# Attention of a decoder layer: 24 instead of 22 head pairs' probabilities turned by DMA, and five steps moved around it

## The reference

```python
x = x + attn(layernorm(x))          # 16 heads of 128; RoPE, causal softmax over 128 keys
x = x + xattn(layernorm(x), k, fside, ctx)   # long convolution of v*ctx with k, skip term, times ctx
x = x + ffn(layernorm(x))           # top 4 of 16 experts (inter 176) and shared experts (704)

scores = einsum('bqnd,bknd->bnqk', Q, K) / sqrt(d_head);  scores = where(causal, scores, -inf)
z = einsum('bnqk,bknd->bqnd', softmax(scores), V);  out = einsum('bqnd,ndm->bqm', z, W_O) + b_O

kv = v[:, :, :, None] * ctx[:, :, None]       # 8 x 8 per group of 8 channels
y = causal_conv(kv, k) + kv * skip
out = einsum('bhijl,bhil->bhjl', y, ctx)
```

## Time and profile before

| | us |
|---|---|
| median of 3 runs (951.35 to 953.11) | 951.75 |
| the profiled execution, its own time | 951.14 |
| its span | 949.3 |
| PE busy / weight load / DVE / ACT / POOL | 896.7 / 797.7 / 789.2 / 454.7 / 502.1 |

### The profile page before, as it was taken

One profiled execution on the slowest core, in us unless ns is written; L12 is line 12 of the kernel. 1 busy time (PEld: TensorE's weight loads), 2 busy tenths in 40 slices (PEclk: granted clock), 3 DMA queues, 4 the chain that ended last, 5 costly groups with the idle time before them and its releaser, 6 DMA issues.

```text
span 949.3 us, 19283 instructions
## 1 busy us (share of the span) xinstructions
PE 896.7 (94%) x6129; PEld 797.7 (84%) x6129; DVE 789.2 (83%) x1706; ACT 454.7 (48%) x1227; POOL 502.1 (53%) x380
## 2 busy tenths in 40 slices
PE   6899999899999989999999999989998799999996
PEld 6798888788889878898887888877887699999985
DVE  6988877878888999788898977876779688888857
ACT  3656645545436564444565333462166244544430
POOL 1443424455554436777363677525718277777760
PEclk9999999999999999999999999999999899999999
DMA  7796371676546754765899575425255277787769
GB/s 271 258 356 232 130 284 72 186 203 144 157 134 189 206 162 133 180 173 179 263 297 290 158 206 133 139 79 221 69 201 161 76 128 131 129 131 132 127 117 310
DMA packets 137345, 169.59 MB, mean 179 GB/s; under 512 B 54944, under 2 KB 112160, under 8 KB 135968
## 3 DMA queue, kind: packets, MB, share of 16 engines
q1 hardware_dynamic: 122800, 149.31, 51.2%
q0 software_dynamic: 14448, 19.05, 12.1%
HBM read 100.52 MB, written 58.44 MB: 167 GB/s over the span
## 4 chain that ended last, share of the span: by engine, by line
PE 64%; DVE 15%; DMA 6%; issue 6%; POOL 4%; ACT 3%; SPq 1%; another core or an unknown queue 0%; DVEq 0%; POOLq 0%; ACTq 0%
PE bank L596 9%; PE bank L598 9%; PE bank L597 8%; PE bank L684 4%; PE bank L913 4%; PE bank L1023 4%; PE bank L710 3%; DVE turn L1612 3%; PE bank L712 3%; PE bank L711 3%; POOL xs L1446 2%; DMA prob_dram<-planes 2%; DVE rot L1633 2%; PE bank L886 2%; PE bank L888 2%
## 5 line engine op out<-in xcount | busy, mean ns | idle before, releaser
L1398 POOL TENSOR_TENSOR z_lo<-prob_t,z_hi 128x512 fp32r<-128x512 f32 x64 | 86.2, 1348 | 218.3 <-ACT z_hi L1257 194.0
L1612 DVE SCALAR_TENSOR_TENSOR turn<-bank,bqk,trig 128x1024 f32<-128x1024 f32 x128 | 161.1, 1276 | 35.5 <-PE bank L598 34.0
L1217 ACT ACTIVATE prob<-prob,negmax 128x128 f32<-128x128 f32 x256 | 99.4, 390 | 123.2 <-DVE negmax L1597 108.0
L1499 POOL DMA_INDIRECT sums<-ysb,token_at x79 | 123.3, 1561 | 57.3 <-DMA sums<-ysb,token_at 29.1
L1439 POOL TENSOR_TENSOR rot<-turn 128x512 f32<-128x512 f32 x64 | 95.2, 1488 | 44.4 <-DVE turn L1612 32.3
L596 PE MATMUL bank<-xt_hi,w_hi 128*128 128x512 f32 x256 | 109.3, 427 | 2.4 <-DVE xt_lo L1574 1.7
L598 PE MATMUL bank<-xt_hi,w_lo 128*128 128x512 f32 x256 | 100.8, 394 | 0.0
L597 PE MATMUL bank<-xt_lo,w_hi 128*128 128x512 f32 x256 | 100.5, 393 | 0.0
L1446 POOL DMA_INDIRECT xs<-xh,dest x64 | 73.7, 1151 | 41.2 <-DVE dest L1780 23.4
L1633 DVE TENSOR_TENSOR rot<-turn 128x512 f32<-128x512 f32 x64 | 92.2, 1480 | 0.0
L1468 POOL TENSOR_TENSOR kv<-c_t,v_t 128x512 f32<-128x512 f32 x60 | 70.5, 1202 | 20.2 <-ACT v_t L1179 11.5
(11 more groups left out here) (200 smaller groups left out, 2537.6 us busy)
## 6 DMA issues: line engine op xcount, KB each, us to landing
w_hi<-w_dram SPq DMA_DIRECT2D x24, 768.0 KB, 5.2
w_lo<-w_dram SPq DMA_DIRECT2D x24, 768.0 KB, 6.6
prob_dram<-planes SPq DMA_DIRECT2D x44, 256.0 KB
xe_all<-xs SPq DMA_DIRECT2D x79, 132.5 KB
wo_hi<-wo_dram SPq DMA_DIRECT2D x26, 256.0 KB, 5.3
wo_lo<-wo_dram SPq DMA_DIRECT2D x26, 256.0 KB, 6.3
sums<-zeros SPq DMA_DIRECT2D x3, 2176.0 KB, 9.6
raw<-in_wqkv SPq DMA_DIRECT2D x16, 384.0 KB, 4.2
```

The source lines that it names most:

```text
L1217: last = nc.scalar.activation(prob[h][:, b, :], prob[h][:, b, :], ACT.Exp, bias=negmax[:, h, b:b + 1], accum_out=total[:, h, b:b + 1])
L1499: nc.gpsimd.indirect_dma_start(sums_dram[s % SUMS], bass.IndirectOffsetOnAxis(ap=token_at[:, s:s + 1], axis=0), ysb[s % YBUFS][:], None, c ...
L1612: last = nc.vector.scalar_tensor_tensor(turn_all[m][:, 2 * i:2 * i + 2, :], qk_bank[2 * m + i][:].unsqueeze(1).to_broadcast([128, 2, GT]), ...
```

## The change

It has these parts:

1. **Two more pairs by DMA**, t = 7 (weighed in step 9) and t = 30 (weighed in step 32, the first of the drain).
2. **Loads behind the turns.** SP issues store, turn, store, turn, then the loads of w and wo.
3. **Skip sums.** The second goes into bank 1, after the projection of QE, instead of bank 5, and the first weighing at p = 3 follows it instead of the projection of QO. QO (bank 1) then waits until DVE has taken it. The wait of the weighing for the skip sums is gone.
4. **Second weighing.** In the steps p = 4 to 7 it comes after QE instead of after KE. In the steps p = 0 to 3 it stays behind KE.
5. **Low parts on POOL.** In steps by DMA head 1's low part comes before both rotations instead of between them.
6. **No wait for the scatters** on POOL (DVE's and SP's own waits for them stay).
7. **The drain step 32.** With pair 30 by DMA, ACT's exponentials of a head come before its weighed values, then a part of the shared experts' weights (`gus_high`); before, they came last. The turn back of the convolution's output (`cross_back`) is made before the scores on PE and added by DVE before the scores' maxima; DVE's low parts of the shared weights come later; SP loads the raw weights after the stores and turns of pair 30.

```diff
 def by_dma(t):
-    return PAIRS <= t < PAIRS * GROUPS - 2
+    return PAIRS - 1 <= t < PAIRS * GROUPS - 1
...
                     if by_dma(t):
-                        prob_store(t, 0)
+                        for h in range(2):
+                            prob_store(t, h)
+                            prob_turn(t, h)
                     if 0 < p < PAIRS - 1:
                         load_w(g, p + 1)
-                    if by_dma(t):
-                        prob_turn(t, 0)
-                        prob_store(t, 1)
-                    if 0 < p < PAIRS - 1:
                         load_o(g, p + 1)
-                    if by_dma(t):
-                        prob_turn(t, 1)
...
+            for h in range(2):
+                prob_store(PAIRS * GROUPS - 2, h)
+                prob_turn(PAIRS * GROUPS - 2, h)
             sp.wait_ge(wo_done, PAIRS * (GROUPS - 1) + W_BEFORE[0] - 1)
             load_wo(0)
             sp.wait_ge(v_ready, 2 * PAIRS * GROUPS)
...
                     pe.wait_ge(prob_landed[h], 16 * (dma_before(t) + 1))
                     if h == 0:
                         pe.wait_ge(v_taken, s * 2 - 2)
-                    if h == 0 and p == 3:
-                        pe.wait_ge(skip_taken, 2 * (s // PAIRS))
...
                 if p == 3:
-                    pe.wait_ge(zt_taken, s * 2 - 4)
                     cross_skip(h, 0, pt_bank)
-                    cross_skip(h, 1, zt_bank)
...
                 if h >= 0 and p == 3:
-                    if i < 2:
-                        pe.wait_ge(vt_taken, 2 * h + i + 1)
-                    elif i == 2:
-                        pe.wait_ge(skip_taken, 2 * h + 1)
+                    if i == 0:
+                        pe.wait_ge(vt_taken, 2 * h + 1)
+                    elif i < 3:
+                        pe.wait_ge(skip_taken, 2 * h + 3 - i)
...
-                    if live(2) and not by_pe and i == int(p == 3) and p < 4:
+                    if by_dma(s - 2) and p == 3 and i == 0:
+                        pe.wait_ge(vt_taken, 2 * g)
+                        cross_skip(g - 1, 1, banks[1])
+                    if by_dma(s - 2) and p < 4 and i == 0:
                         weigh_values(s, p, 0, first)
-                    if live(2) and not by_pe and i == 2:
+                    if by_dma(s - 2) and i == (2 if p < 4 else 0):
                         weigh_values(s, p, 1, first)
...
                         exps(h)
                         take_weighed(h)
                         weighed_high(h)
+                        if g == GROUPS:
+                            gus_high(h)
...
                 if late:
                     first_probs(s)
+                    z_low(s, 1)
                 for m in range(2):
-                    if late and m:
-                        z_low(s, 1)
...
                     ).then_inc(scattered[g], 16)
-                pool.wait_ge(scattered[g], 16 * hi)
...
                 if g == GROUPS and p == 0:
                     tokens_again(0)
-                    gus_low(0)
+                    cross_add(h - 1)
...
                 if p == 0 and g == GROUPS:
-                    cross_add(h - 1)
                     dve.wait_ge(back_added, 2 * (GROUPS - 1))
                     token_moments(2 * GB, 3 * GB)
+                    gus_low(0)
                     gus_low(1)
```

More of the change, by code:

```diff
@@ L73, in by_dma @@
 def by_dma(t):
-    return PAIRS <= t < PAIRS * GROUPS - 2
+    return PAIRS - 1 <= t < PAIRS * GROUPS - 1
 def dma_before(t):
-    return min(max(t - PAIRS, 0), PAIRS * (GROUPS - 1) - 2)
+    return min(max(t - PAIRS + 1, 0), PAIRS * (GROUPS - 1))
 def pe_before(t):
@@ L746, in between_weighings @@
                 s, h = g * PAIRS + p, g - 1
-                if p == 0 and g == GROUPS:
-                    two_banks_free(g, p, live)
-                    pe.wait_ge(v_taken, s * 2 - 1)
-                    cross_back(h - 1)
                 if g == 0 or not live(0):
@@ L892, in step @@
                     last.then_inc(wo_done, 1)
-                if p == 0 and 1 < g < GROUPS:
+                if p == 0 and g > 1:
                     two_banks_free(g, p, live)
                     pe.wait_ge(v_taken, s * 2 - 1)
-                    cross_back(h - 1)
+                    cross_back(g - 2)
                 beside_first(g, p, live)
@@ L1268, in step @@
                         h = i % 2
-                        if i == 1 and g == GROUPS and p < 2:
-                            if p == 1:
-                                root((g - 2) * GB, (g - 1) * GB)
-                            gus_high(2 * p)
-                            if p == 0:
-                                gus_high(1)
+                        if i == 1 and g == GROUPS:
+                            root((g - 2) * GB, (g - 1) * GB)
+                            gus_high(2)
                         if i == 3 and g == GROUPS and p == 1:
@@ L1921, in beside_scored @@
                     cross_skip(h, 0, pt_bank)
-                    cross_skip(h, 1, zt_bank)
+                    cross_skip(h, 1, banks[1])
                 if p >= 4:
```

## The result

The changed kernel takes 962.88 us (median of 8 runs, 959.58 to 967.62) against 953.82 for the kernel before (950.32 to 958.16), a ratio of 1.010 (95% interval 1.008 to 1.012): 1% slower, where 12 us less were forecast (range 935 to 948 us). Its profiled execution took 962.59 us, span 960.8; that of before is 11.5 us shorter. Single executions of one kernel lie several us apart, so times are compared by ratios and causes by the traces' own steps.

What follows compares the result with a forecast made beforehand. The prediction took PE as the bound, with DVE close behind. Its terms, -11.5 - 2.5 + 1.0 - 1.0 + 0.5 + 1.5 = -12.0 us, gave 939.1 us profiled, 939.7 median, range 935 to 948.

Steps and rivals of the forecast that it cites:

- What bounds the kernel: Groups 1 and 2: PE sets the pace, busy 157.1 of 162 and 154.8 of 160 us, DVE close behind.
- Loads behind the turns, no scatter wait, low part first, -11.5: Steps by DMA: PE's turn and output-sum stalls, 13.8 us, vanish; 11.5 us gained, bounds 5 to 13.8.
- The rule of the Trainium skill: DMA turns: 1309 ns per block against 390 on TensorE, 10.5 us a turn; the prediction trusted the trace's 3.23 us.
- Second weighing, -2.5 and +1.0: Steps p = 4 to 7: PE's wait before QO filled, 2.5 us gained; ACT slipping in some steps, 1.0 lost.
- Pair 7, -1.0: Pair 7 turned by DMA: two PE transpositions removed, 1.0 us gained, bounds 0 and 2.
- Skip sums, +0.5: At p = 3: QO waits for DVE's skip product instead of the weighing; 0.5 us lost, between 0 and 1.5.
- The drain, +1.5, at worst +5: Step 32 to the next output sum: 1.5 us lost, between a gain of 1 and a loss of 5.
- Rival C: Rotations: POOL and DVE hold each other up, 1.9 us a step, kernel 6 us slower, 958 us; chance 0.08.
- Rival A: DVE takes over: PE's gain mostly becomes waits for DVE; -7 us, 944.8 us; chance 0.22.
- B: Turns land no earlier: 8.5 us of stalls stay, about 7 of the 11.5 lost; 946.7 us; chance 0.05.

Runs made afterwards that it cites:

- b_mix2: Kernel before without POOL's scatter wait, the three zero fills moved ahead of group 1's steps, weight loads behind both turns; 941.50 us, ratio 0.988.
- a_drain: Changed kernel with its drain as before (pair 30 turned by TensorE, step 32 in its old order); 953.93 us, ratio to before 0.999.
- m_drain: b_mix2 with the changed kernel's drain (pair 30 by DMA, raw shared weights behind its turns); 953.65 us, ratio to before 1.002.
- b_mix: Kernel before without POOL's scatter wait and with the three zero fills moved ahead of group 1's steps; 947.09 us, ratio 0.992.
- m_low: b_mix2 with POOL's second low part ahead of both rotations; 951.60 us, ratio to before 0.999.
- a_fill: Changed kernel with the three zero fills issued in group 2 instead of group 3; 964.51 us, ratio to before 1.011.

## Why the prediction was wrong

- *What bounds the kernel.* Right that TensorE has the pace and DVE is close. Missed: POOL, busy for half of the time, has no room either from its division to its first kv. Its share of busy time hid that.
- *Loads behind the turns, no scatter wait, low part first, -11.5.* This step failed. It summed stalls that vanish, each from its own row, and took the covers as free. Measured one by one on before: loads +0.7%, no scatter wait -0.6%, low part +0.8%. The sentence "the rotations end at most as much later as the weighed values of head 1 come after the first rotation" had the delay right; it then looked only at the scores, and not at kv and the convolution behind the rotations. The sentence "the loads go out some 5 us later, for the next step" named no queue behind them: the next pair's store, the scattered rows, and the fills of group 3, which the prediction never named. Two of the three edits are a gain of 1.2% if the fills are moved as well and the low part stays. That these 12 us equal the forecast's sum is chance: they hold the fills, which it never named, and 2 us of the drain.
- *The rule of the Trainium skill* ("VectorE: DVE Perf Modes", The three transpose paths). The measured turns bear the row out, not the page's figure: in b_mix2 no turn of 22 pairs was waited for. What made a turn late was what lay in front of its store.
- *Second weighing, -2.5 and +1.0.* Failed: ACT did not slip, and zc's 3.0 us did go, but the steps p = 5 and 6 got 0.26 longer, since QO, now behind the weighing, brought DVE's reciprocals and with them POOL's division a quarter of a microsecond later. Alone it is worth nothing (1.001), on b_mix2 it costs 4 us.
- *Pair 7, -1.0.* No gain shows: steps p = 0 to 2 of group 1 took 50.17 us with it and without it.
- *Skip sums, +0.5.* Right in kind: QO waits for the same product. The size hangs on the clock: on b_mix2, where it fell behind the wait, step 32 began 1.7 us later; at a clock of 1.00 the p = 3 step of group 2 got 0.6 us shorter.
- *The drain, +1.5, at worst +5.* Failed: some 10 us undone (a_drain, by the ratios), 12 added (m_drain). The chain was written along ACT, and the term took the low part as free to follow the high part. It is the second low part's place behind the division, through DVE's low parts of the raw weights, that set the end (4.1 us), with ACT's wait for the raw weights (2.05). These went out 5.7 us later against the step's scores, as forecast; that they are "due at ACT when they are about to land" was 2 us short. The granted clock that fell behind the idle stretch was in no term.
- *Rival C* had its sign: the division's mean rose by 45% (1.09 to 1.59 us, from 138 to 612 us; the rows of before and of after stand below) and the loss came with it. DVE's rotations kept their time (1.57 and 1.56 us), so its price, 1.9 us a step, was wrong. Its place was right in part: at p = 2 the room before the scores did take the longer division, but the work of p = 3 behind it had no such room, nor had p = 1; in the other steps the low part costs by POOL's kv. *Rival A* held in part: at p = 1 to 3 what TensorE gained was waited out for DVE. *B* had its sign, 7.1 of the 8.5 us still there, but not its cause: in 5 places instead of 12, and gone in b_mix2, where no fill lies in front.

```profile
L1621 DVE TENSOR_TENSOR prob<-prob,rtotal 128x512 f32<-128x512 f32 x24 | 26.2, 1093 | 0.8
```

```profile
L1612 DVE TENSOR_TENSOR prob<-prob,rtotal 128x512 f32<-128x512 f32 x24 | 38.1, 1587 | 0.8
```

Left open: what part of the 10 us of the drain is clock. No run took the wait away and kept the clock, or the other way round.

## What to carry to other kernels

An instruction that is moved ahead on an engine moves everything between its old and its new place back; follow each of these to who waits for it, also on an engine with a low share of busy time, since a half idle engine can be the bound in one stretch of each step. A transfer that is moved behind another is in front of the next one: name that one, and add the bytes issued between. Stalls in rows can't be summed over edits that share a queue or an order; here the loads behind the turns were worth +0.7% alone and -0.5% beside two other edits (b_mix to b_mix2).

## What the runs showed of the hardware

- A multiply of 128x512 f32 on VectorE (the division) took 0.68 to 1.83 us from 138 to 612 us, and its mean followed the order of GpSimd's work beside it: 1.03 us where GpSimd had a low part between two rotations (b_mix2), 1.62 where these stood back to back (m_low).
- With 2 MB of loads and a fill of 2.2 MB issued ahead, the issue of a 256 KB store took 4.43 us itself, not 0.4, and its turn could go 10.7 us behind it; all DMA together moved 342 GB/s on the mean of 494 to 507 us.
- Idle time of TensorE was followed by a lower clock: behind the drain's waits the granted clock was 0.71 for 20 us, where it had been 1.00, and a weight load of the output sum took 0.33 us instead of 0.19. The length of the wait alone did not decide it: behind 3.3 us before QO the clock fell in the changed kernel (24.87 us for the step) and not in a_fill (23.52, group 3), and in the kernel before it stayed behind a wait of 2.87 us and fell behind one of 2.67.
